# A value unit of sequence 1 moved ahead of transpose 10, and two value units moved ahead of projections 2 and 3 of sequence 0

## What is computed

```
x = x + attn(layernorm(x), ...)          # x: (16, 512, 512)
x = x + ffn(layernorm(x), w1, b1, w2, b2)

attn: q, k, v, o = x@Wq.T, x@Wk.T, x@Wv.T, x@Wog.T     # v: "value units"
      i, f = soft_cap(x@Wig.T + big), soft_cap(x@Wfg.T + bfg)
      h = mlstm_scan(q, k, v, i, f)                    # 8 heads
      y = (sigmoid(o) * multihead_norm(h, gamma)) @ Wout.T   # "projections"
ffn:  out = gelu(x @ ternary(w1).T + b1) @ ternary(w2).T + b2
```

## Time and profile before

| | us |
|---|---|
| median of three runs | 1740.55 (1740.52 to 1741.01) |
| the profiled execution, its own time | 1742.3 |
| its span in the trace | 1740.6 |
| TensorE busy | 1707.5 (98%) |
| VectorE busy | 1437.6 (83%) |
| ScalarE busy | 1059.6 (61%) |
| GpSimd busy | 606.6 (35%) |

### The profile page before, as it was taken

The page is one execution under the profiler, slowest core; times in us unless marked ns, Lnnn a source line. Parts: engine busy times, 40 slices in busy tenths (PEclk is TensorE's granted clock), DMA queues, the critical chain, the costliest instruction groups (busy, mean ns, idle before and its releaser), DMA issues.

```text
span 1740.6 us, 31380 instructions
## 1 busy us (share of the span) xinstructions
PE 1707.5 (98%) x12028; PEld 841.4 (48%) x12028; DVE 1437.6 (83%) x2528; ACT 1059.6 (61%) x1769; POOL 606.6 (35%) x477
## 2 busy tenths in 40 slices
PE   6899999999999999999999999999999999999999
PEld 4554445444444444445444444444444444454455
DVE  7888788897888978789887888988789788886872
ACT  6978375473746638375573746648375573847643
POOL 1242514335241442514235241442514235241430
PEclk9999999999999999999999999999999999999999
DMA  8736253442725326253442725336262442625120
GB/s 321 219 89 167 58 141 72 117 120 56 170 60 127 87 80 160 58 154 59 120 117 56 171 60 126 87 92 152 55 161 61 110 119 56 148 59 132 33 55 25
DMA packets 294981, 187.45 MB, mean 108 GB/s; under 512 B 239136, under 2 KB 260640, under 8 KB 289712
## 3 DMA queue, kind: packets, MB, share of 16 engines
q1 hardware_dynamic: 293248, 182.30, 41.7%
q10 hardware_dynamic: 1584, 3.15, 0.5%
HBM read 96.47 MB, written 20.23 MB: 67 GB/s over the span
## 4 chain that ended last, share of the span: by engine, by line
PE 81%; DVE 8%; DMA 3%; SPq 3%; issue 2%; POOL 1%; ACT 1%; POOLq 0%; DVEq 0%; ACTq 0%
PE pf L2073 24%; PE pf L2057 22%; PE pa L1926 17%; PE pa L1902 7%; PE psh L1926 5%; SPq L530 2%; PE psh L2013 2%; DMA kT<-shared 1%; PE psh L1968 1%; PE psh L2047 1%; DVE gT L1633 1%; PE pa L2013 1%; DVE dec L1482 1%; PE pa L1893 1%; PE psh L2009 1%
## 5 line engine op out<-in xcount | busy, mean ns | idle before, releaser
L2073 PE MATMUL pf<-w2T,gT 128*128 128x512 f16 x2048 | 505.8, 379 | 0.0
L2057 PE MATMUL pf<-x2T,w1T 128*128 128x512 f16 x1920 | 422.0, 379 | 0.0
L2057 PEld LDWEIGHTS pf<-x2T,w1T 128*128 128x128 f16 x1920 | 185.4, 98 | 222.5
L2073 PEld LDWEIGHTS pf<-w2T,gT 128*128 128x128 f16 x2048 | 195.5, 97 | 177.0
L1633 DVE SCALAR_TENSOR_TENSOR gT<-g,wscale,gT 128x512 f16<-128x512 f32 x240 | 208.5, 871 | 22.5 <-ACT gT L1046 20.2
L1926 PE MATMUL pa<-wT,xT 128*128 128x512 f16 x960 | 212.8, 379 | 0.6 <-ACT sig L970 0.6
L1043 ACT ACTIVATE g<-pf,b1c 128x512 f32<-128x512 f32 x240 | 164.1, 684 | 72.5 <-PE pf L2057 56.6
L1046 ACT ACTIVATE gT<-g,wscale 128x512 f16<-128x512 f32 x240 | 173.3, 722 | 7.9
L1926 PE MATMUL pa<-wT,shared 128*128 128x512 f16 x768 | 176.2, 379 | 1.6 <-DMA shared<-qT 0.8
L1051 ACT ACTIVATE ktok<-kT 128x512 f32<-128x512 f32 x64 | 40.4, 631 | 216.4 <-DVE kT L1528 214.9
L1902 PE MATMUL pa<-xT,wT 128*128 128x512 f16 x768 | 171.4, 379 | 0.0
(11 more groups left out here) (246 smaller groups left out, 2705.2 us busy)
## 6 DMA issues: line engine op xcount, KB each, us to landing
dec<-gate_r SPq DMA_DIRECT2D x32, 1024.0 KB, 6.1
xin<-L_attn_x SPq DMA_DIRECT2D x16, 1024.0 KB, 6.0
out<-x1b SPq DMA_DIRECT2D x64, 256.0 KB, 2.3
xres<-L_attn_x SPq DMA_DIRECT2D x16, 512.0 KB, 4.3
xres<-L_attn_x SPq DMA_DIRECT2D x32, 256.0 KB, 3.0
qw<-gate_w SPq DMA_DIRECT2D x128, 48.0 KB, 2.0
s<-state_w SPq DMA_DIRECT2D x60, 97.5 KB, 2.4
qw<-kT SPq DMA_DIRECT2D x120, 48.0 KB, 2.0
```

The source lines that it names most:

```text
L2057: last = nc.tensor.matmul(bank, w1T[:, k, tok(f)], x2T[:, part, :, k, :], start=(k == 0 and part == HI), stop=(k == KD - 1 and part == LO))
L2073: last = nc.tensor.matmul(bank, gT[:, part, f, tok(t)], w2T[:, f, :], start=(f == 0 and part == HI), stop=(f == NF - 1 and part == LO), sk ...
```

## The change

- ScalarE: `ternary_out(9)` goes ahead of `squares(0, 2)`; in its old place stands `value(1, 1)`, which reads bank `pf[:, 1]` in place of `ps[:, 1]`; `gates(1)` no longer has it.
- TensorE: in place of 18 fillers there are 5, then value unit 1 of sequence 1 into `pf[:, 1]`, then transpose 10; transpose 11 has a new wait, for ScalarE's copy of that unit. Behind transpose 15 come value unit 0 and now value units 2 and 3 of sequence 1, and then projections 2 and 3 of sequence 0. In `sequence(1, 0, True)` the two late value units are gone from the head.

```diff
@@ scalar: gates(b, fb)
                 gate_log(b)
-                value(b, 1)
+                if not (isinstance(b, int) and b == 1):
+                    value(b, 1)
                 value(b, 2)
@@ scalar: value(b, t)
-                    bank, free = ps[:, 1, :], ps_free[1]
+                    bank, free = pf[:, 1, :] if isinstance(b, int) and b == 1 else ps[:, 1, :], ps_free[1]
@@ scalar: sequence
                     ternary_out(8)
                     small2_gone(12)
+                    ternary_out(9)
                 squares(b, 2)
                 if not run_f:
                     weights_hi(*USES_OUT[2:4])
                 gated_hi(b, 1)
                 if not run_f:
-                    ternary_out(9)
+                    value(1, 1)
                     small2_gone(13)
                     ternary_out(10)
@@ tensor: sequence
                 if first:
                     opening()
-                else:
+                elif not (isinstance(b, int) and b == 1):
                     late_values(b, 2)
                     late_values(b, 3)
@@ tensor: first_heads
                 weights_out(2, 3)
-                busy_until(10, 18)
+                pe.wait_ge(pf_free[0], 5)
+                keep_busy(pf[:, 0, :], 5)
+                x_ready(1)
+                pe.wait_ge(ps_free[1], at(1, PS_USES[1], 0))
+                pe.wait_ge(pf_free[1], 5)
+                token_products(pf[:, 1, :], xT[:, :, 1, :, :], C_V).then_inc(ps_fill, 1)
+                ternary_transpose(10)
+                pe.wait_ge(ps_free[1], at(1, PS_USES[1], 1))
                 ternary_transpose(11)
                 weights_ready(*USES_OUT)
                 project(0, 0)
                 ternary_transpose(12)
                 project(0, 1)
                 ternary_transpose(13)
-                x_ready(1)
                 gates(1)
                 ternary_transpose(14)
                 ternary_transpose(15)
-                late_values(1, 1)
                 tokens(1, U_V, xT[:, :, 0, :, :], C_V)
+                late_values(1, 2)
+                late_values(1, 3)
                 project(0, 2)
                 project(0, 3)
```

## The result

The changed kernel takes 1743.07 us (median of 20 runs, 1741.06 to 1744.74); the kernel before, in runs beside it, 1740.53 us (20 runs, 1739.36 to 1741.91). The ratio is 1.0013, with a 95% interval of 1.0007 to 1.0019: 2.5 us slower, between 1.2 and 3.3. That is within 0.2% of no change, inside the range of the prediction (1740.0 to 1743.8), and 1.0 us more than the 1.49 us that was forecast.

What follows compares the result with a forecast made beforehand. A rigid TensorE matmul train carries early shifts to the end. Part 1 gains nothing; part 2's 3.35 us gain turns idle, and projection 3's 1.83 less 0.34 slack gives +1.49: 1740.55 to 1742.0 us, range 1740.0 to 1743.8.

Steps and rivals of the forecast that it cites:

- a late handover: ScalarE's copy of value unit 1 late beyond 0.31 us of slack, bounded by 1.01 us; upper bound of shift +2.5 us.
- rival C: Value unit does not fit the fillers' place; copy 1.01 us late, projection 3 0.5 to 0.7 later, 1742.6 us; chance 0.08.
- What bounds the kernel: Behind the first sequence, a rigid train of TensorE matmuls: a microsecond won or lost near 100 to 135 us reaches the total.
- the waits behind 160 us: Sign of being wrong: TensorE's waits in the later sequences change by more than 1 us.
- Part 1: Value unit 1 replaces 13 of 18 fillers (2.81 us) from 94.81 us; gain up to transpose 15 set at nothing.
- the unit prices: TensorE, 123.78 to 131.55 us: unit of 12 matmuls 2.59 us, one 512-column matmul 0.216 us, at full clock.
- Part 2, projection 3: New TensorE order behind transpose 15: projection 3 at 117.84 us, 1.83 later, moving the VectorE and ScalarE chain by 1.83.
- The shift of query 1: Query 1 starts at 133.29 instead of 131.80 us: +1.49, the 1.83 of projection 3 less 0.34 of slack.
- Rival A: Chain behind projection 3 does not bind; keys, query and `gate_columns` run without idle time, gain 3.35 us, 1737.2; chance 0.07.
- Rival B: Clock falls in the new idle time near 126 to 133 us, costing up to 3.4 us: 1745.4 us; chance 0.08.

Runs made afterwards that it cites:

- The third profile: The changed kernel, unaltered, profiled a third time: no clock fall, `outer(1)` 1.40 us later than in the kernel before; no separate median given.
- part 2 alone: Against the kernel before: values 2 and 3 ahead of projections 2 and 3, with the 18 fillers and value unit 1 left in place; 1745.27 us, ratio 1.0027.

## Why the prediction was right or wrong

The range and the forecast of no change held; the likeliest time, 1742.0, was 1.0 us low. That 1743.07 lies within 1743.8 is in part luck: the upper end was made of a late handover and of rival C, which did not occur, and not of the clock, which did.

- *What bounds the kernel.* Right. Behind `outer(1)` every profile runs at 104.11 us a sequence; what was lost near 133 us is found in the end. One sign of being wrong was met in the letter: the waits behind 160 us changed by more than 1 us (1.9 to 0.4 in the first pair of profiles). It was too narrow a sign, since three profiles of the changed kernel alone differ by 0.9.
- *Part 1.* Right, to 0.1 us: value unit at 94.80 in the frame (94.81 forecast), transpose 11 at 98.25 (98.3), transpose 15 as before by the 13.75 us from the fillers on. ScalarE's squares had 0.23 us to spare. Projection 0 was 0.1 later in the first profile and at 99.17 as before in the other two, and that did not reach transpose 15. One reading goes further than its row: the earlier trace rows have the full clock for 92 to 96 us alone; that it held in the stretch of the unit prices, up to 131.55, is shown by the same profile, which has 1.00 from 80 to 150 us.
- *Part 2, projection 3.* Right: 117.84 in the frame, as forecast. VectorE's late arguments end at 130.23 (130.22), `keys(1, 1)` at 133.14 (133.14), `gate_columns` at 131.63 (131.6).
- *The shift of query 1.* 1.39 us where 1.49 was forecast: TensorE woke 0.05 us after ScalarE and not 0.15. The third profile, with no fall, has the same 1.39, and `outer(1)` there 1.40 later, covered as forecast. So the chain is shown: it stands in all three profiles, part 2 alone makes it 2.59 longer, and moving one ScalarE copy takes it away.
- *Rival A* is excluded: `gate_columns` waited for ScalarE in every profile of the changed kernel. *Rival C* too: transpose 11 was in time.
- *Rival B* is the step that failed, in its chance and in its size. It was given 0.08, since query 0 stood between the idle times; it happened in three of five profiles with that pattern, and by the mean clocks in 22 of 32 executions of the changed kernel. And it was priced at 3.4 us, from the 6.8 us of the earlier trace rows; where it came, it lasted 3.4 us and cost 1.6 to 1.7. Seven tenths of that is about the 1.0 us by which 2.5 exceeds 1.49. So the forecast of the likeliest case was that of an execution without the fall (1742.0; those six have a median of 1741.79), and the median of all lies between the two kinds. B's own time, 1745.4, was too high by the same mis-sizing: with the measured 1.7 it would have been 1743.7, and the 14 with the fall have 1743.35.
- *The rule of the Trainium skill* (TensorE: Matmul & The Clock Gate, Why this matters for your kernels), against idle gaps between bursts of matmuls, is meant there for gaps longer than any of the three here, which the prediction left out; taken by the words of that section it gives no fall. The measurement decides: gaps of 1.8, 1.3 and 1.1 us close together were followed by one in three profiles of five.

## What to carry to other kernels

When fillers are replaced by work from later on, ask first what the fillers were waiting for: TensorE can only use the time if the other engines' chain gets shorter too, and a unit that is pulled ahead of a chain's head (projection 3 here) pushes the chain back. Count the units between the head of the chain and the instruction that needs its end; here five covered it, four (one value unit in place of two) covered it as well, and three did not. And idle time is not priced at its own length: in this kernel three short idle times close together brought a fall of the clock in most executions. Fillers set into them cost nothing here, because each group was shorter than its gap, and there was no fall with them.

## What the runs showed of the hardware

- The granted clock can fall or stay with the same pattern of idle times: 1.8, 1.3 and 1.1 us with twelve matmuls between the first two gave a fall in three profiles of five, and in the changed kernel a mean clock of 0.994 or less in 22 of 32 executions; 3.0 us in one piece gave none in its one profile, though 7 of that kernel's 11 executions have the low mean; 2.2 us with full matmuls on both sides gave one in the second profile of the kernel before. A single profile is not enough to say what a gap costs.
- Each of the four falls behind 80 us lasted 3.4 us, and cost 1.6 to 1.7 us; the one between 69 and 80 us lasted 6.8 us in every profile.
- With 15 fillers of 0.216 us set into those idle times the clock was at 1.00 in the profile and no execution of 11 had the low mean; query 1 stood at the same place to 0.01 us.
- One transposing DMA of the same shape landed after 3.45 us in one execution and after 5.07 in another; SP took 7.2 to 8.5 us to issue the same four transposes over fourteen profiles.
